# Reciprocals of the attention denominators by way of DRAM instead of spread products, and output stores on another queue

## The chip, the cores and the metric

One core of one Trainium2 chip runs the kernel. The metric is the device time of one execution in microseconds (us). The kernel before took 2346.55 us (median of 3 runs, 2340.79 to 2351.91).

## What is computed

The input is 8 images of 256 channels and 48x48 pixels, in fp32. The first layer is an attention over pixels with 8 heads and a residual (phase L0 of the kernel). The second layer is a linear attention of 64 heads of 8 channels: 32 heads on a 1x1 projection of the image, 32 on that projection after a 5x5 depthwise convolution and a grouped 1x1 product. Cut to what matters here:

```python
qkv = einsum('oc,bchw->bohw', w_qkv, x)
qkv_ms = concatenate([qkv, aggreg(qkv, w_dw, w_pw)], axis=1)     # two sources of 32 heads
q, k, v = relu(...), relu(...), ...                              # per head, 8 channels each
vk  = einsum('bhdn,bhen->bhde', [v, 1], k)
out = einsum('bhde,bhen->bhdn', vk, q)
out = out[:, :, :-1] / (out[:, :, -1:] + 1e-15)                  # one denominator per head and pixel
y = einsum('oc,bchw->bohw', w_proj, out)
result = batch_norm(y) * gamma + beta + x                        # statistics over all 8 images
```

## The kernel before

Three phases follow one another, each a block with one instruction stream per engine: `phase_l0` (the first layer), `phase_l1` (all of the second but its normalisation), `phase_out` (batch norm, residual, store). The change is in the last two.

`phase_l1` takes the images in order, and each image in six units u = 0 to 5, one per part (k, v or q) and half of the heads. On TensorE a unit is: eight groups `convolve(i, u, j)` of 12 matmuls (the convolution with the grouped product folded into its weights `wc`), eight pairs `project(i, u+2)` for the unit two ahead, and after units 1 to 3 of every image but the first `output(i-1, ...)`, the projection of the previous image, 32 matmuls for two chunks of 384 pixels. VectorE makes the weights `wc` of a unit just before that unit (`weights`, in two halves, from `taps`), and in between computes products of k and v (`spin`). ScalarE empties PSUM.

The attended values are never formed: q is divided by its denominator and then multiplied by one matrix `mt1` that holds vk and the projection. Denominators of image i-1 are made during units 0 of image i: `denominators(i-1, d)` for d = 0, 1, 2, each for two chunks of pixels, puts 128 rows of denominators (4 groups of 32) into the PSUM bank `ao`. `reciprocals` on VectorE turns them into `rcp` (two buffers of 384 columns). Every row must then reach the 8 rows of its head in q. In the kernel before TensorE does that: ScalarE rounds `rcp` to `rhi`, GpSimd makes the rest `rlo = rcp - rhi`, and `spread_out` multiplies a 0/1 matrix `spread` with `rhi` and `rlo`, two matmuls of 384 columns for each of 24 tiles (6 chunks x 4 groups of q rows). `normalize` on VectorE multiplies q by each tile in PSUM. The table `SPREADS` says where they stand: 8 of the 24 pairs between the projections c = 5 to 7 of unit 0, and two behind each convolution group of unit 1. `output` waits for all 24.

SyncE (SP) issues all DMAs of this phase in one order written out by hand: per unit the taps, `lay_store` (convolution results to DRAM in two halves), `lay_load` (back to SBUF in head order), `replicate` (projection of the unit two ahead to DRAM, a wait for its landing, and 2.6 MB back as `rep`), and `store_y`. All waits are on semaphores, in the order of the program of each engine.

After the last image, `denominators`, `reciprocals`, `spread_out` and `output` run with nothing beside them but SP's early loads for the last phase (lines 709 to 712). `phase_out` keeps five buffers; SP loads y and x1 of an image, ScalarE scales, VectorE adds, and GpSimd's queue stores (line 1262) as soon as the sum is there.

Of the kernel before, what the change touches and what calls it, by code (L numbers as in the profile page):

```python
# [11 lines left out]
P = 128  # L12
# [13 lines left out]
NU = 6  # L26
# [488 lines left out]
def phase_l1(nc, dram, sem, bnst, q, x1, work, early):  # L515
# [3 lines left out]
    with ExitStack() as ctx:  # L519
# [3 lines left out]
        def ps(name, shape):  # L523
# [9 lines left out]
        spread = sb("spread", [P, 2, 4, P], F32R)  # L533
# [11 lines left out]
        rhi = sb("rhi", [P, 2, CHUNK], F32R)  # L545
        rlo = sb("rlo", [P, 2, CHUNK], F32R)
# [13 lines left out]
         bc_filled, bc_freed, q_copied, rhi_ready, rlo_ready, spread_ready, y_filled, y_freed, bn_done, y_out) = (  # L560
# [4 lines left out]
                "bc_filled bc_freed q_copied rhi_ready rlo_ready spread_ready y_filled y_freed bn_done y_out").split())  # L565
# [3 lines left out]
        NFIRST, NW = 1, 5  # L569
# [5 lines left out]
        SPREADS = {(0, 5): range(0, 2), (0, 6): range(2, 5), (0, 7): range(5, 8),  # L575
                   **{(1, j): range(8 + 2 * j, 10 + 2 * j) for j in range(NG)}}

        spread_raw = stage.rearrange("p h j n -> p (h j n)")[:, 0:8 * P].rearrange("p (c j h) -> p c j h", c=2, j=4)

# [26 lines left out]
        def bc_bank(i, k):  # L606

            return (cv if i is last_image and k % 4 >= 2 else tr)[:, k % 2]
# [17 lines left out]
        def _(sp):  # L626
# [4 lines left out]
            sp.dma_start(spread_raw, dram["spread"]).then_inc(w_in, 16)  # L631
# [17 lines left out]
            def lay_store(i, u):  # L649

                for h in range(2):
# [18 lines left out]

            def image(i, nxt):
# [43 lines left out]
        def _(pe):  # L715
# [105 lines left out]
            def spread_out(i, ks):  # L821

                for k in ks:
                    c, j = k // 4, k % 4
                    d = c // 2
                    if k % 8 == 0:
                        pe.wait_ge(rhi_ready, i * NDEN + d + 1)
                        pe.wait_ge(rlo_ready, i * NDEN + d + 1)
                    if i is last_image:
                        wait_count(pe, bc_freed, 4 * NCH * i + (k - 3 if k >= 4 else 0))  # L830
                    else:
                        if k == 0:
                            pe.wait_ge(tr_freed, (i + 1) * NTR + DG)
                        wait_count(pe, bc_freed, 4 * NCH * i + (k - 1 if k >= 2 else 0))
                    nc.tensor.matmul(bc_bank(i, k)[:, :CHUNK], spread[:, c % 2, j, :], rhi[:, d % 2, :],
                                     start=True, stop=False)
                    nc.tensor.matmul(bc_bank(i, k)[:, :CHUNK], spread[:, c % 2, j, :], rlo[:, d % 2, :],  # L837
                                     start=False, stop=True).then_inc(bc_filled, 1)

            def output(i, chunks, u):  # L840


                pe.wait_ge(bc_freed, 4 * NCH * (i + 1))
# [3 lines left out]
                for c in chunks:  # L847
                    for m in range(CT):
                        k = 2 * c + m
                        if c >= chunks[0] + 2:  # L850
                            pe.wait_ge(y_freed, 2 * NCH * i + k - 3)
                        for j in range(4):
                            mm = nc.tensor.matmul(y_bank(k)[:, :CHUNK], mt[:, j, m * P:(m + 1) * P],  # L853
                                                  q[:, j, c * CHUNK:(c + 1) * CHUNK], start=(j == 0), stop=(j == 3))
                        mm.then_inc(y_filled, 1)

            def image(i, prev, nxt):


                for u in range(NU):  # L860
                    if u == 0 and not prev:
                        product(i, 0, range(DG))
                    for j in range(NG):
# [9 lines left out]
                        if u == 1 and prev:  # L873
                            spread_out(i - 1, SPREADS[u, j])
# [12 lines left out]
                    for c in range(NG):  # L887
                        if u + 2 < NU or nxt:
                            project(*unit_at(i, u + 2), [c])
                        if u == 0 and prev:  # L890
                            if c == 1:
                                denominators(i - 1, 2)
                            spread_out(i - 1, SPREADS.get((u, c), ()))
# [10 lines left out]
            pe.wait_ge(spread_ready, 1)  # L904
# [8 lines left out]
            spread_out(last_image, range(8))  # L913
            denominators(last_image, 2)
            spread_out(last_image, range(8, 4 * NCH))
# [3 lines left out]
        def _(act):  # L919
# [55 lines left out]
            def round_reciprocals(i, d):  # L975

                act.wait_ge(r_ready, i * NDEN + d + 1)

                wait_count(act, bc_filled, 4 * NCH * i + (8 if d == 2 else 0))
                nc.scalar.copy(rhi[:, d % 2, :], rcp[:, (d % 2) * CHUNK:(d % 2 + 1) * CHUNK]).then_inc(rhi_ready, 1)  # L980

# [18 lines left out]
            def image(i, prev, nxt):  # L1000


                for u in range(NU):
                    if u == 0 and not prev:
                        product(i, 0, range(DG))
                    for j in range(NG):
# [7 lines left out]
                        if u == 1 and j == 0 and prev:  # L1014
                            round_reciprocals(i - 1, 2)
# [12 lines left out]
                    for c in range(NG):  # L1028
                        if u + 2 < NU or nxt:
                            project(*unit_at(i, u + 2), [c])  # L1030
                        if u == 0 and prev and c in (0, 3):
                            round_reciprocals(i - 1, c // 3)
# [13 lines left out]
            nc.scalar.copy(spread[:], spread_raw).then_inc(spread_ready, 1)  # L1046
# [6 lines left out]
            for d in range(NDEN):  # L1053
                round_reciprocals(last_image, d)
# [3 lines left out]
        def _(pool):  # L1058
# [24 lines left out]
            def attend(i):  # L1083

                for d in range(NDEN):
                    pool.wait_ge(rhi_ready, i * NDEN + d + 1)

                    wait_count(pool, bc_filled, 4 * NCH * i + (8 if d == 2 else 0))
                    nc.gpsimd.tensor_tensor(rlo[:, d % 2, :], rcp[:, (d % 2) * CHUNK:(d % 2 + 1) * CHUNK],
                                            rhi[:, d % 2, :].bitcast(F32), ALU.subtract).then_inc(rlo_ready, 1)  # L1090

            for i in range(NIMG):
                if i:
                    masked(i - 1, 3)
                    attend(i - 1)
# [3 lines left out]
            attend(last_image)  # L1099

        @block.vector
        def _(dve):
# [48 lines left out]
            def reciprocals(i, d):  # L1151
                dve.wait_ge(den_filled, i * NDEN + d + 1)
                wait_count(dve, rlo_ready, i * NDEN + (1 if d == 2 else 0))
# [5 lines left out]
            def normalize(i, ks):  # L1159
                for k in ks:  # L1160
                    c, j = k // 4, k % 4
                    dve.wait_ge(bc_filled, 4 * NCH * i + k + 1)
                    qc = q[:, j, c * CHUNK:(c + 1) * CHUNK]
                    nc.vector.tensor_tensor(qc, qc, bc_bank(i, k)[:, :CHUNK], ALU.mult).then_inc(bc_freed, 1)  # L1164
# [12 lines left out]
            def image(i, prev):  # L1177
# [33 lines left out]
            reciprocals(last_image, 0)  # L1211
            reciprocals(last_image, 1)
            normalize(last_image, range(8))
            reciprocals(last_image, 2)
            normalize(last_image, range(8, 4 * NCH))
            statistics(last_image, range(NCH))


def phase_out(nc, dram, sem, bnst, q, x1, early):

    with ExitStack() as ctx:
# [36 lines left out]
        @block.gpsimd  # L1258
        def _(pool):
            for k in range(NIMG):  # L1260
                pool.wait_ge(summed, k + 1)
                pool.dma_start(dram["out"][order[k]], buffers[k % NB][0]).then_inc(store[k % NB], 16)
            for r in range(NB):
                pool.wait_ge(store[r], 16 * len(range(r, NIMG, NB)))

        @block.scalar
        def _(act):
            act.wait_ge(stat, CT + 1)
            nc.scalar.activation(rt[:], ve[:], ACT.Sqrt).then_inc(root, 1)
            act.wait_ge(stat, CT + 9)  # L1270
            for k in range(NIMG):
# [5 lines left out]
                last.then_inc(scaled, 1)  # L1277

# [50 lines left out]
def layouts(inputs):  # L1329
# [49 lines left out]
    j = np.arange(4)  # L1379
    row, half = k[:, None, None, None], NB * np.arange(2)[None, :, None, None]  # L1380
    out["spread"] = ((row // 32 == j[None, None, :, None]) & (row % 32 == half + group[j // 2])).astype(np.float32)
# [23 lines left out]
```

## Time and profile before

| what | value |
|---|---|
| profiled execution, its own time | 2353.07 us |
| span of its instructions | 2351.3 us |
| median of three runs | 2346.55 us |
| PE / DVE / ACT / POOL busy | 91% / 65% / 35% / 9% |
| mean granted TensorE clock | 0.955 |
| DMA, hardware queues / GpSimd's queue, share of 16 engines | 51.1% / 1.9% |

Times inside the profile are us from the span's start. In the profile PE is TensorE's matmuls, PEld its weight loads, DVE VectorE, ACT ScalarE, POOL GpSimd, SP SyncE, and L745 is line 745 of the kernel before. The granted clock is a share of 2.4 GHz.

### The profile page before, as it was taken

How to read it: one execution, taken by the hardware profiler on the slowest of the kernel's cores; microseconds unless marked ns; L12 is line 12 of the kernel's file. 1: busy time of each engine (PE TensorE's matmuls, PEld its weight loads, DVE VectorE, ACT ScalarE, POOL GpSimd, SP SyncE). 2: the span in 40 equal slices, each digit the busy share in tenths (PEclk: the TensorE clock that was granted, in tenths of full speed). 3: DMA queues.
4: the chain of work that ended last, by engine and by line, in shares of the span. 5: the costliest groups of instructions: out<-in, count | busy, mean ns of one | idle time of the engine just before them, and what ended most of it. 6: DMA issues, size and time to landing. Idle time of an engine off the chain costs nothing. (4 is left out here: it accounts for less than half of the span.)

```text
span 2351.3 us, 31988 instructions
## 1 busy us (share of the span) xinstructions
PE 2133.4 (91%) x12680; PEld 1513.9 (64%) x12680; DVE 1530.9 (65%) x2330; ACT 833.4 (35%) x1807; POOL 214.3 (9%) x207
## 2 busy tenths in 40 slices
PE   6999999999698799999999999999999999999810
PEld 6888888889566466666666656666666665665500
DVE  4667766767418849667676794975866679491452
ACT  4434434344233333332342332333333233333142
POOL 2233122331100000000000000000000000000000
PEclk9999999999899899999999999999999999999865
DMA  2201222020376864865686486486577658646578
GB/s 105 81 41 41 81 81 81 1 81 41 126 265 214 289 213 159 287 229 209 231 279 213 181 277 224 173 285 226 197 255 254 206 190 270 223 176 222 231 324 358
DMA packets 137411, 448.14 MB, mean 191 GB/s; under 512 B 6960, under 2 KB 105904, under 8 KB 119216
## 3 DMA queue, kind: packets, MB, share of 16 engines
q1 hardware_dynamic: 136112, 427.24, 51.1%
q0 software_dynamic: 1152, 18.87, 1.9%
q8 instruction: 101, 1.65, 0.3%
q14 instruction: 46, 0.38, 0.0%
HBM read 271.30 MB, written 174.78 MB: 190 GB/s over the span
## 5 line engine op out<-in xcount | busy, mean ns | idle before, releaser
L745 PE MATMUL cv<-work,wc 128*64 128x288 f32 x4608 | 620.4, 414 | 22.6 <-issue 18.4
L745 PEld LDWEIGHTS cv<-work,wc 128*64 128x64 f32 x4608 | 307.7, 137 | 267.9 <-issue 53.3
L726 PE MATMUL pj<-x,wqkv 128*128 128x288 f32 x1536 | 389.4, 410 | 20.3 <-DMA x<-scratch_x 20.3
L726 PEld LDWEIGHTS pj<-x,wqkv 128*128 128x128 f32 x1536 | 288.7, 191 | 114.0 <-issue 39.8
L1130 DVE STREAM_SHUFFLE spun<-work 128x1152 f32<-128x1152 f32 x240 | 345.2, 1444 | 0.1
L955 ACT ACTIVATE work<-cv 128x288 f32<-128x288 f32 x384 | 158.0, 411 | 514.6 <-PE cv L745 508.9
L1136 DVE SCALAR_TENSOR_TENSOR spun<-work,spun 128x1152 f32<-128x1152 f32 x240 | 321.2, 1343 | 0.0
L1111 DVE TENSOR_TENSOR wc<-taps 128x512 f32<-128x512 f32 x288 | 180.3, 689 | 194.9 <-PE cv L745 182.4
L936 ACT COPY work<-pj 128x288 f32<-128x288 f32 x384 | 153.6, 400 | 289.5 <-PE pj L726 288.9
L1164 DVE TENSOR_TENSOR q<-q,tr 128x384 f32<-128x384 f32 x180 | 92.2, 550 | 93.8 <-PE tr L837 93.8
L853 PE MATMUL cv<-q,mt 128*128 128x384 f32 x384 | 127.9, 486 | 1.0 <-DVE q L1164 1.0
L853 PE MATMUL tr<-q,mt 128*128 128x384 f32 x384 | 127.8, 486 | 0.0
L199 PE MATMUL qv<-whi,xhi 128*128 128x512 f32 x288 | 117.1, 407 | 0.0
L781 PE MATMUL tr<-ident,work 128*128 128x128 f32 x708 | 115.2, 284 | 1.5 <-ACT spread L1046 1.5
L762 PE MATMUL vk<-kvT 128*128 128x129 f32 x708 | 113.2, 284 | 1.5 <-ACT kvT L967 0.3
L408 POOL TENSOR_TENSOR qs<-qs,qrc 128x512 f32<-128x512 f32 x72 | 75.2, 1049 | 428.4 <-DVE qrc L458 428.4
L201 PE MATMUL qv<-whi,xlo 128*128 128x512 f32 x288 | 113.2, 393 | 0.0
L781 PEld LDWEIGHTS tr<-ident,work 128*128 128x128 f32 x708 | 78.9, 142 | 53.1 <-issue 51.5
L200 PE MATMUL qv<-wlo,xhi 128*128 128x512 f32 x288 | 112.4, 390 | 0.0
L1077 POOL TENSOR_TENSOR vkm<-mask,vkd 128x128 f32<-128x128 f32 x15 | 6.7, 447 | 1141.8 <-DVE vkd L1149 1141.8
L199 PE MATMUL kx<-qnhi,mthi 128*128 128x256 f32 x288 | 91.3, 317 | 16.1 <-DVE mtlo L500 16.0
L853 PEld LDWEIGHTS tr<-q,mt 128*128 128x128 f32 x384 | 73.0, 190 | 50.9
(112 smaller groups left out, 2996.8 us busy)
## 6 DMA issues: line engine op xcount, KB each, us to landing
work<-scratch_padded SPq DMA_DIRECT2D x48, 2599.5 KB, 10.6
scratch_padded<-work SPq DMA_DIRECT2D x48, 1300.0 KB, 6.5
scratch_phases<-work SPq DMA_DIRECT2D x96, 576.0 KB, 5.1
work<-scratch_phases SPq DMA_DIRECT2D x64, 576.0 KB, 5.2
x<-scratch_x SPq DMA_DIRECT2D x9, 2304.0 KB, 10.4
scratch_x<-xs SPq DMA_DIRECT2D x8, 2304.0 KB, 6.9
q<-scratch_phases SPq DMA_DIRECT2D x32, 576.0 KB, 4.6
xs<-in_x SPq DMA_DIRECT2D x7, 2304.0 KB, 9.1
```

Source lines behind the costliest of these rows:

```text
L199: nc.tensor.matmul(out, lhi, rhi, start=start, stop=False, skip_group_check=True)
L201: return nc.tensor.matmul(out, llo, rhi, start=False, stop=stop, skip_group_check=True)
L726: mm = nc.tensor.matmul(pj[:, c % 2, :PLANE], wqkv[:, kc, u, :], x1[:, kc, c * PLANE:(c + 1) * PLANE], start=(kc == 0), stop=(kc == CT - 1))
L745: mm = nc.tensor.matmul(cv[64 * b:64 * b + 64, j % 2, :PLANE], wc[:, 2 * j + b, dy].rearrange("p c o -> p (c o)"), window, start=(dy == 0) ...
L762: mm = nc.tensor.matmul(vk[:, 0:P + 1], kvT[:, g % 2, 0, t, 0:P], kvT[:, g % 2, 1, t, :], start=(g == 0 and t == 0), stop=(g == last and t ...
L781: mm = nc.tensor.transpose(tr[:, g % 2, (2 * kv + t) * P:(2 * kv + t + 1) * P], src, ident[:])
L853: mm = nc.tensor.matmul(y_bank(k)[:, :CHUNK], mt[:, j, m * P:(m + 1) * P], q[:, j, c * CHUNK:(c + 1) * CHUNK], start=(j == 0), stop=(j == 3))
L936: nc.scalar.copy(inner(u % 2, c), pj[:, c % 2, :PLANE].rearrange("p (r c) -> p r c", c=PX)).then_inc(pj_freed, 1)
L955: nc.scalar.activation(stage[:, j // 4, j % 4], cv[:, j % 2, :PLANE], ACT.Copy if PARTS[u] == 2 else ACT.Relu).then_inc(cv_freed, 1)
L1111: op = nc.vector.tensor_tensor(wc[:, blocks, dy], taps[:, u % 2, blocks, 0:DIM].rearrange("p g (c o) -> p g c o", o=1).to_broadcast([P, HB ...
L1130: nc.vector.stream_shuffle(spun[:, t % 2], vc[:, piece], SPINS[t % DIM]).then_inc(spun_ready, 1)
L1136: nc.vector.scalar_tensor_tensor(out=spun[:, t % 2], in0=kc[:, piece], scalar=1.0, in1=spun[:, t % 2], op0=ALU.mult, op1=ALU.mult, accum_o ...
```

## The change

`spread`, `rhi`, `rlo`, the two operations that make them, `spread_out` and `SPREADS` are gone, with the load of the matrix at the start. `normalize` now multiplies q by SBUF tiles of 1536 columns, 6 per image (two groups of q rows by two chunks each) instead of 24 of 384. The tiles come through DRAM: SP stores each `rcp` in two halves into `scratch_recip`, laid out head by head, and loads it with every head's row repeated for its 8 channels. In steady state there are two tiles, `bcb`; for the last image tiles 2 to 5 lie in tensors no longer needed. In `phase_out` the stores are issued by ScalarE, each behind the scaling of the next image; the SBUF that GpSimd's DMAs reserve is cut to 256 bytes.

```diff
+            def store_reciprocals(i, d):
+                sp.wait_ge(r_ready, i * NDEN + d + 1)
+                wait_count(sp, bc_freed, NCH * i)
+                for source in range(2):
+                    sp.dma_start(dram["recip"][d, source].rearrange("h r n -> r h n"),
+                                 rcp[64 * source:64 * source + 64, (d % 2) * CHUNK:(d % 2 + 1) * CHUNK]).then_inc(rc_out[d], 16)
+
+            def load_reciprocals(i, n):
+                d, source = n // 2, n % 2
+                sp.wait_ge(rc_out[d], 32 * (i + 1))
+                if i != last_image:
+                    wait_count(sp, bc_freed, NCH * i + (n - 1 if n >= 2 else 0))
...
+                rows, tile = dram["recip"][d, source], bc_tile(i, n)
+                if source == 0:
+                    sp.dma_start(tile, bass.AP(rows.tensor, rows.offset, [[0, DIM], [4 * CHUNK, NB], [1, 4 * CHUNK]])
+                                 ).then_inc(bc_in[n], 16)
+                else:
+                    for h in range(2):
+                        sp.dma_start(tile[h:P:2], bass.AP(rows.tensor, rows.offset + HB * h * 4 * CHUNK, [
+                            [4 * CHUNK, HB], [0, DIM], [1, 4 * CHUNK]])).then_inc(bc_in[n], 16)
@@ SP, image(i)
-                    lay_store(i, u)
+                    lay_store(i, u, [0])
+                    if u == 1 and i:
+                        load_reciprocals(i - 1, 4)
+                        load_reciprocals(i - 1, 5)
+                    lay_store(i, u, [1])
...
+                    if u == 0 and i:
+                        for d in range(NDEN):
+                            store_reciprocals(i - 1, d)
+                        load_reciprocals(i - 1, 0)
+                        load_reciprocals(i - 1, 1)
...
                     if u + 2 < NU or nxt:
                         replicate(*unit_at(i, u + 2))
+                    if u == 0 and i:
+                        load_reciprocals(i - 1, 2)
+                        load_reciprocals(i - 1, 3)
@@ SP, after the last image, ahead of the early loads
+            for d in range(NDEN):
+                store_reciprocals(last_image, d)
+                load_reciprocals(last_image, 2 * d)
+                load_reciprocals(last_image, 2 * d + 1)
@@ PE, output
-                pe.wait_ge(bc_freed, 4 * NCH * (i + 1))
...
+                    pe.wait_ge(bc_freed, NCH * i + 2 * (c // 2 + 1))
@@ DVE
-            def normalize(i, ks):
...
+            def normalize(i, ns):
+                for n in ns:
+                    d, source = n // 2, n % 2
+                    dve.wait_ge(bc_in[n], (16 + 16 * source) * (i + 1))
+                    qc = q[:, 2 * source:2 * source + 2, d * 2 * CHUNK:(d + 1) * 2 * CHUNK]
+                    nc.vector.tensor_tensor(qc, qc, bc_tile(i, n).rearrange("p (j n) -> p j n", j=2), ALU.mult
+                                            ).then_inc(bc_freed, 1)
@@ DVE, image(i)
-                    normalize(i - 1, range(12))
                 weights(i, 1, [1])
                 if prev:
-                    normalize(i - 1, range(12, 4 * NCH))
+                    normalize(i - 1, range(NCH))
                 weights(i, 2)
@@ phase_out, ACT
+            def store_out(k):
+                act.wait_ge(summed, k + 1)
+                act.dma_start(dram["out"][order[k]], buffers[k % NB][0]).then_inc(store[k % NB], 16)
...
                 last.then_inc(scaled, 1)
+                if k:
+                    store_out(k - 1)
+            store_out(NIMG - 1)
```

## Rows read from the trace of the kernel before

**Rows 1.** The profile's page: busy time by engine; granted clock in 40 slices.
```profile
PE 2133.4 (91%) x12680; PEld 1513.9 (64%) x12680; DVE 1530.9 (65%) x2330; ACT 833.4 (35%) x1807; POOL 214.3 (9%) x207
...
PEclk9999999999899899999999999999999999999865
```

**Rows 2.** Busy time in one image; last three figures: granted clock, DMA share, GB/s.
```profile
858.30:1052.20 193.90, 193.14 (x1143) 122.16 (x1141) 139.97 (x210) 66.10 (x173) 5.66 (x12) 1.00 0.67 230
```

**Rows 3.** Groups by line: shapes, count | busy us, mean ns | idle before, releaser.
```profile
L1164 DVE TENSOR_TENSOR q<-q,tr 128x384 f32<-128x384 f32 x180 | 92.2, 550 | 93.8 <-PE tr L837 93.8
...
L835 PE MATMUL tr<-rhi,spread 128*128 128x384 f32 x180 | 73.7, 410 | 8.1 <-DVE q L1164 6.3 <-issue 1.8
...
L837 PE MATMUL tr<-rlo,spread 128*128 128x384 f32 x180 | 61.4, 341 | 0.0
...
L1307 DVE TENSOR_TENSOR work<-work 128x4608 f32<-128x4608 f32 x4 | 19.7, 4956 | 23.2 <-ACT work L1276 23.2
```

**Rows 4.** Timeline of PE, image 1: start us, us, engine, line, operation, count.
```profile
854.51 4.15 PE L726 MATMUL pj<-x,wqkv 128*128 128x288 f32 x16
858.28 0.55 PE L835 MATMUL tr<-rhi,spread 128*128 128x384 f32 x1
...
864.45 1.68 PE L745 MATMUL cv<-work,wc 128*64 128x288 f32 x12
...
884.35 7.92 PE L726 MATMUL pj<-x,wqkv 128*128 128x288 f32 x32
892.11 5.32 PE L853 MATMUL cv<-q,mt 128*128 128x384 f32 x16
...
902.63 1.68 PE L745 MATMUL cv<-work,wc 128*64 128x288 f32 x12
...
944.65 11.88 PE L745 MATMUL cv<-work,wc 128*64 128x288 f32 x96
```

**Rows 5.** Timeline of DVE in the same stretch.
```profile
855.24 2.55 DVE L1157 RECIPROCAL work<-work 128x384 f32<-128x384 f32 x1
...
885.14 3.70 DVE L1111 TENSOR_TENSOR wc<-taps 128x512 f32<-128x512 f32 x6
891.72 0.01 DVE L1130 LOAD_MASK_SELECT spun<-work  x1 [2.89 <-DMA work<-scratch_phases]
```

**Rows 6.** Timeline of SP's DMA issues in the same stretch.
```profile
848.26 3.31 SPq L668 DMA_DIRECT2D work<-scratch_phases  x2
863.36 0.37 SPq L640 DMA_DIRECT2D scratch_padded<-work  x1
869.42 0.53 SPq L646 DMA_DIRECT2D work<-scratch_padded  x1
```

**Rows 7.** DMA issues of the run: count, KB each, median us to landing.
```profile
work<-scratch_padded SPq DMA_DIRECT2D x48, 2599.5 KB, 10.6
...
scratch_y<-q SPq DMA_DIRECT2D x21, 768.0 KB, 8.2
...
wkqv<-in_wkqv SPq DMA_DIRECT2D x1, 768.0 KB, 4.3
```

**Rows 8.** Busy time by stretch, columns as in Rows 2: one behind an idle TensorE, one of early loads.
```profile
801.20:815.70 14.50, 14.50 (x97) 8.44 (x97) 14.33 (x22) 2.88 (x7) 0.00 (x0) 0.81 0.83 286
...
2190.00:2200.00 10.00, 7.81 (x40) 4.77 (x44) 9.84 (x12) 1.02 (x2) 2.00 (x2) 0.71 1.01 431
```

**Rows 9.** Timeline of PE: idle us before, and its releaser, in brackets.
```profile
654.69 1.06 PE L781 MATMUL tr<-ident,work 128*128 128x128 f32 x8 [1.48 <-ACT spread L1046]
...
801.19 14.51 PE L745 MATMUL cv<-work,wc 128*64 128x288 f32 x96 [12.28 <-issue]
...
1796.04 2.81 PE L745 MATMUL cv<-work,wc 128*64 128x288 f32 x12 [2.68 <-DMA work<-scratch_padded]
...
2211.88 5.43 PE L853 MATMUL cv<-q,mt 128*128 128x384 f32 x16 [1.02 <-DVE q L1164]
```

**Rows 10.** Timeline of the end: SP's first early load, ScalarE's last scaling.
```profile
2187.03 0.34 SPq L710 DMA_DIRECT2D work<-scratch_y  x1
...
2333.06 4.50 ACT L1276 ACTIVATE work<-work,sh,sc 128x2304 f32<-128x2304 f32 x2 [10.89 <-DMA work<-scratch_x]
```

More of the change, by code:

```diff
@@ L544, in phase_l1 @@
         mt = sb("mt1", [P, 4, C])
-        rhi = sb("rhi", [P, 2, CHUNK], F32R)
-        rlo = sb("rlo", [P, 2, CHUNK], F32R)
+        bcb = sb("bcb", [P, 2, 4 * CHUNK])
         spun = sb("spun", [P, 2, SPIN])
@@ L568, in phase_l1 @@
         lay_stored, lay_done = ((lay_stored0, lay_stored1), (lay_stored2, lay_stored3)), ((lay_done0, lay_done1), (lay_done2, lay_done3))
-        NFIRST, NW = 1, 5
+        rc_out = [sem(f"l1_rc_out{d}") for d in range(NCH // 2)]
+        bc_in = [sem(f"l1_bc_in{n}") for n in range(NCH)]
+        NFIRST, NW = 1, 4
         last_image = NIMG - 1
@@ L604, in groups_of, with bc_tile @@
             return DG if PRODUCTS[p][1] == 0 else AG
-        def bc_bank(i, k):
-            return (cv if i is last_image and k % 4 >= 2 else tr)[:, k % 2]
+        def bc_tile(i, n):
+            if i == last_image and n >= 2:
+                spare = (wc.rearrange("p b y c o -> p (b y c o)"), spun.rearrange("p t n -> p (t n)"),
+                         wqkv.rearrange("p k u m -> p (k u m)"))[0 if n < 4 else n - 3]
+                first = (n % 2) * 4 * CHUNK if n < 4 else 0
+                return spare[:, first:first + 4 * CHUNK]
+            return bcb[:, n % 2]
         def y_bank(k):
@@ L647, in replicate, with lay_store @@
                     rows.tensor, rows.offset, [[NB * PADDED, P // 2], [1, 2], [1, NB * PADDED - 1]])).then_inc(rep_in[u % 2], 16)
-            def lay_store(i, u):
-                for h in range(2):
+            def lay_store(i, u, halves=range(2)):
+                for h in halves:
                     sp.wait_ge(cv_freed, i * (NU * NG) + u * NG + 4 * (h + 1))
@@ L819, in denominators @@
                 mm.then_inc(den_filled, 1)
[L821 to L838, printed above, removed]
             def output(i, chunks, u):
-                pe.wait_ge(bc_freed, 4 * NCH * (i + 1))
                 if u is not None:
@@ L1045, in _ @@
             act.wait_ge(w_in, 16 * NW)
-            nc.scalar.copy(spread[:], spread_raw).then_inc(spread_ready, 1)
             image(0, False, True)
@@ L1052, in _ @@
             project_product(last_image, 3)
-            for d in range(NDEN):
-                round_reciprocals(last_image, d)
             output(last_image, range(NCH))
@@ L1210, in _ @@
                 image(i, True)
[L1211 to L1216, printed above, removed]
+            for d in range(NDEN):
+                reciprocals(last_image, d)
+            for d in range(NDEN):
+                normalize(last_image, range(2 * d, 2 * d + 2))
+                if d:
+                    statistics(last_image, range(2 * d - 2, 2 * d))
+            statistics(last_image, range(NCH - 2, NCH))
 def phase_out(nc, dram, sem, bnst, q, x1, early):
@@ L1256, in _ @@
                 sp.dma_start(x, dram["x1"][order[k]]).then_inc(loaded, 16)
[L1258 to L1264, printed above, removed]
         @block.scalar
         def _(act):
+            def store_out(k):
+                act.wait_ge(summed, k + 1)
+                act.dma_start(dram["out"][order[k]], buffers[k % NB][0]).then_inc(store[k % NB], 16)
             act.wait_ge(stat, CT + 1)
@@ L1277, in _ @@
                 last.then_inc(scaled, 1)
+                if k:
+                    store_out(k - 1)
+            store_out(NIMG - 1)
+            for r in range(NB):
+                act.wait_ge(store[r], 16 * len(range(r, NIMG, NB)))
         @block.vector
@@ L1378, in layouts @@
     out["headsel"] = (group.T[:, :, None, None] + NB * np.arange(2)[:, None] == np.arange(32)).astype(np.float32)
-    j = np.arange(4)
-    row, half = k[:, None, None, None], NB * np.arange(2)[None, :, None, None]
-    out["spread"] = ((row // 32 == j[None, None, :, None]) & (row % 32 == half + group[j // 2])).astype(np.float32)
     return {n: np.ascontiguousarray(v) for n, v in out.items()}
@@ L1398 @@
     dram["phases"] = nc.dram_tensor("scratch_phases", (2, NG, P, PLANE), F32).ap()
+    dram["recip"] = nc.dram_tensor("scratch_recip", (NCH // 2, 2, NB, 4, CHUNK), F32).ap()
     dram["out"] = nc.dram_tensor("out_0", (NIMG, P, CT, HW), F32, kind="ExternalOutput").ap()
```

44 lines of the change are left out of this document (8 added, 36 removed).

## The prediction

> **What bounds the kernel now.** I read the page first: TensorE is busy 91% of the span and its granted clock is at the upper level almost throughout, so it sets the time [rows 1]. Then busy time by image: the period is 193.9 us and PE is busy for 193.1 of it, DVE for 140, and the DMA engines are busy 0.67 of it, 230 GB/s [rows 2]. So a microsecond taken from PE in the second phase is worth one, as long as DVE and the transfers still arrive before PE asks. How late they may be is read from the timelines, below. The last 100 us are another thing: PE has ended, and ScalarE's last scaling waits for a DMA [rows 10].
>
> **What the change removes from PE.** 8 spread pairs stand between projections in unit 0, 16 between convolutions in unit 1. Unit 1: the eight groups of convolutions run from 864.45 to 884.35, 19.90 us; the same 96 matmuls with nothing between take 11.8 (944.65, 11.88) [rows 4]: 8.1 us. Unit 0: from 858.28 to 864.45, 6.17 us, only two of the eight projection pairs are left, and eight in a row take 7.92, so 1.97 for two [rows 4]: 4.2. Together 12.3 us per image, seven images, 86 us (the durations of the two lines add to 135, since matmuls overlap [rows 3]). Unhindered, PE would come to unit 2 of image 1 at 902.63 - 12.3 = 890.3.
>
> **What it removes and adds elsewhere.** DVE: 24 products of 0.55 (13.2 us) [rows 3] become 6 of 1536 columns; the sums of 4608 columns take 4.96, so 1.65 each, 9.9 in all, with no wait for PE between. ScalarE and GpSimd lose three short operations per image; neither bounds anything there. SP gains 6 stores (96 KB each) and 9 DMAs that load 6 tiles of 768 KB per image, 4.7 MB, some 13% more bytes than the image's 230 GB/s x 193.9 us = 44.6 MB read and written; engines busy 0.67 have room. It is not the room but the order that costs.
>
> **The cost of one load.** No row shows a load like it: all transfers before have 64 or 128 rows as the outermost count on both sides, the new ones 8 on the DRAM side (and 4 for the stores). Lower bound: `wkqv`, the same 768 KB in the same rows of 6144 bytes, landed in 4.3 us with nothing ahead [rows 7]; at the 431 GB/s of a full queue [rows 8] its bytes are 1.8 of that, the other 2.5 fixed. Upper bound: the y stores, 768 KB amid the image's traffic, 8.2 [rows 7], so 5.7 of transfer. Neither row is plainly nearer: one has the shape of the row, the other the company. I take the middle, 3.7.
>
> A rule of the Trainium skill speaks here: "DMA: Bandwidth & Descriptors", section "Why a DMA increments its semaphore by 16 and not by 1", says that a DMA is spread over the largest number of engines, up to 16, that divides the outermost count of both sides. That is 8 engines for these loads; 8 of 16 at 431 GB/s make 3.65 us of transfer, an estimate by that page that falls on the middle. Were all 16 used it would be 1.8, the first rival. No run here shows it yet.
>
> **The chain of waits in image 1.** Transfers of SP are taken to run one behind the other.
> - Reciprocals 2 are ready at 857.8 [rows 5]. SP, free since 851.6 [rows 6], has waited for them; its two stores (0.37 each) end at 858.5. Transfers start about 1 us later, half a microsecond for the stores (0.2 at full rate to 1.8), so load 0 moves 860.0 to 863.7, load 1 to 867.4, and they are in SBUF 1.5 later. Products 0 and 1 end at 870.5; `output` wants them at 879.9. Covered.
> - `replicate` of unit 2, issued at 863.36 and landed at 869.42 before [rows 6], now stands behind 1.5 MB: landed at 872.2. The load of `rep` (10.6 [rows 7], some 9.3 to its last byte) moves until 881.5.
> - Loads 2 and 3 are issued behind it: last bytes 885.2 and 888.9; products 2 and 3 end at 888.3 and 892.0.
> - SP then waits for these, since tile 4 takes the buffer of tile 2: load 4 is issued at 888.4, stands behind the taps and a `lay_store` (0.8 MB, 2.0 us) and moves 890.9 to 894.6; load 5 to 898.3, landed 899.8, product 5 ends at 901.5.
> - DVE is in order: `weights(i, 2)` stood at 885.14 [rows 5]. Now its first half ends at 901.5 + 1.9 = 903.4. PE, there at 890.3, waits 13.1 us.
> - After an idle of 12.28 us 96 matmuls took 14.51 instead of 11.88, at a granted clock of 0.81, that is, part of it at the lower level, 1.2 GHz [rows 8, 9]; after 2.68 idle, 12 took 2.81 instead of 1.68 [rows 9]. I add 2.7.
>
> So unit 2 starts effectively at 903.4 + 2.7 = 906.1 instead of 902.63 [rows 4]: +3.5 us per image, +24.5 for seven. With 1.8 of transfer the same chain gives 892.9 + 1.1 = 894.0, -8.6 per image; with 5.7, 915.4 + 2.7, +15.5.
>
> Queued behind SP's waits for products 2 and 3: the second half of `lay_store` (unit 1), its `lay_load` and `replicate` of unit 3. The kva data then land at about 905 instead of 891.7 [rows 5], just when DVE is ready for `spin`; `weights(i, 3)` follows 32 us of DVE work later, at 938, while PE asks for it 42 us after unit 2's start (944.65 - 902.63 [rows 4]), at 948. Covered, by 10 us; later units keep their distance, as nothing in them changes.
>
> **Start, end and last phase.** Start: the matrix is not loaded and rounded, for which PE waited 1.48 [rows 9]; -1. After the last image store, load and product are a bare chain instead of rounding and spreading. Output began at 2211.88 [rows 9]; the first two tiles allow it at about 2208, but tiles 2 and 3 come at 2220 and 4 and 5 at 2231, where PE asked for their chunks before at 2222 and 2232: 0. With 1.8 of transfer it is 8 earlier, less 2 of clock. The early loads stood in SP's program at 2187.03 [rows 10] and now stand behind load 5: issued at about 2220, 11.8 MB at 431 GB/s [rows 8], done at 2255, where the last phase starts at 2245 and is bound by DMA: +8 (0 with fast loads). There a store is issued only behind the scaling of the next image, so stores 4 to 6 no longer stand before loads that ScalarE waits for (2333.06 [rows 10]); each is 5.5 us of transfer; some of it comes back at the end, where the last stores queue up: -5 (0 to -8). Sum +2.
>
> Total: +24.5 + 2, about +27. The profiled execution was 2353.07, 6.5 above the median of the runs; from the median, 2346.55 + 27 = 2373.
>
> **Rivals.**
> 1. Loads at full rate (1.8): 7 x -8.6 - 6 - 5 - 1, about -72: 2275. One mechanism: the chain through load 5 ends near 893, so PE waits only 3 us; it decides below about 3.1 us of transfer, where the chain costs what the spreads saved. For it: rows and bytes as in `wkqv`, which is the only row of this row length. Against it: the outermost counts. Chance 0.25.
> 2. The chain and the saving cancel: transfer near 3.1, or part of the queueing overlaps: 2335 to 2358. For it: DMA engines that idle between waits catch up; against: every link is a true dependence. 0.18.
> 3. Loads as slow as the y stores (5.7), since six of them meet `rep` and the taps: +108 and +10: 2465. Against it: those 8.2 us contain waiting of their own. 0.09 for anything over 2410.
>
> The forecast has 0.48, and its own range is 2358 to 2410.
>
> **How the numbers follow.** Half a per cent, 12 us, is about what can be told from no change. Faster: rival 1 and a little of 2, 0.27; same: 0.18; slower: the forecast and rival 3, 0.55. Leaving out the outer half of rival 1 and most of rival 3 gives 2290 to 2410.
>
> **What would show it.** PE: convolutions of unit 1 at 1.475 us each with nothing between, and an idle of 10 to 15 us before unit 2, put down to `wc` (DVE L1111), a granted clock below 1.00 behind it. DMA issues: `bcb<-scratch_recip` at 6 to 8 us from issue to landing. DVE: waits for that DMA before products 2 to 5, of 1.65 each. If the idle before unit 2 is under 5 us, the load was mis-sized and the first rival holds; if PE waits elsewhere, at `output` or unit 3, the chain was drawn wrong; if the last phase starts its loads at 2245 unhindered, the term of +8 falls.

## The result, and the profile after

The changed kernel took 2504.26 us (median of 4 runs, 2500.18 to 2508.97) against 2346.59 for the kernel before (4 runs, 2340.79 to 2351.91): ratio 1.067, 95% interval 1.065 to 1.069. The forecast was 2373, the range ended at 2410. The direction was right, the size far off: +158 us instead of +27.

The page after: busy time by engine, then the granted clock in 40 slices and the DMA packets by size. Rows 1 answer to it.
```profile
span 2507.2 us, 31140 instructions
...
PE 2061.4 (82%) x12296; PEld 1460.1 (58%) x12296; DVE 1515.2 (60%) x2186; ACT 823.9 (33%) x1782; POOL 186.9 (7%) x175
...
PEclk9999999999899979989997997999899799899755
...
DMA packets 147248, 490.04 MB, mean 195 GB/s; under 512 B 7712, under 2 KB 109728, under 8 KB 129056
```
TensorE has 72 us less to do than in [rows 1] and the span is 156 longer. The lines say where it waits: groups of instructions after (count | busy, mean ns | idle before, releaser).
```profile
L787 PE MATMUL cv<-work,wc 128*64 128x288 f32 x4608 | 620.8, 418 | 221.9 <-issue 221.0 <-DMA work<-scratch_padded 0.7
...
L1156 DVE TENSOR_TENSOR q<-q,bcb 128x1536 f32<-128x1536 f32 x44 | 77.4, 1758 | 313.7 <-DMA bcb<-scratch_recip 313.7
```
The convolutions stand idle for 222 us, and VectorE waits 314 us for the new loads: 7.1 us before each of 44 products. The timeline of TensorE, image 1, answers to [rows 4]:
```profile
859.00 11.88 PE L787 MATMUL cv<-work,wc 128*64 128x288 f32 x96
...
888.99 0.27 PE L834 MATMUL ao<-ident,vkm 128*128 128x128 f32 x1
914.52 3.15 PE L787 MATMUL cv<-work,wc 128*64 128x288 f32 x12 [25.26 <-issue]
...
940.93 7.92 PE L768 MATMUL pj<-x,wqkv 128*128 128x288 f32 x32
```
Unit 1 runs its 96 convolution matmuls in 11.88 us with nothing between, TensorE is at unit 2 at 889.3, and there it waits 25 us. The profile names "issue" as the releaser, which here only says that no semaphore event was matched; VectorE's timeline (next) shows what it is: the weights of unit 2 begin at 912.53. Image 1 is the best of the seven:
```profile
1132.92 3.15 PE L787 MATMUL cv<-work,wc 128*64 128x288 f32 x12 [33.45 <-issue]
...
2199.20 3.15 PE L787 MATMUL cv<-work,wc 128*64 128x288 f32 x12 [30.99 <-issue]
```
The seven idles before unit 2 sum to 202.5 us. In the kernel before, unit 2 of the last image starts at 2071.80:
```profile
2071.80 1.68 PE L745 MATMUL cv<-work,wc 128*64 128x288 f32 x12
```
From the starts of unit 2 the 156 us of span add up: 914.52 against 902.63 [rows 4] in image 1 is +11.9; the six periods up to 2199.20 sum to 1284.7 against 1169.2, +115.5; the rest to the end is 308.0 against 279.5, +28.5.

VectorE after, image 1 (start, duration, line, operation, idle before and releaser); [rows 5] answer to it.
```profile
856.03 0.56 DVE L1147 TENSOR_SCALAR work<-ao 128x384 f32<-128x384 f32 x1 [3.33 <-DMA scratch_recip<-work]
856.62 2.55 DVE L1149 RECIPROCAL work<-work 128x384 f32<-128x384 f32 x1
859.09 1.82 DVE L1103 TENSOR_TENSOR wc<-taps 128x512 f32<-128x512 f32 x3
869.49 1.76 DVE L1156 TENSOR_TENSOR q<-q,bcb 128x1536 f32<-128x1536 f32 x1 [8.57 <-DMA bcb<-scratch_recip]
873.23 1.76 DVE L1156 TENSOR_TENSOR q<-q,bcb 128x1536 f32<-128x1536 f32 x1 [1.99 <-DMA bcb<-scratch_recip]
893.57 1.76 DVE L1156 TENSOR_TENSOR q<-q,bcb 128x1536 f32<-128x1536 f32 x1 [18.58 <-DMA bcb<-scratch_recip]
898.05 1.76 DVE L1156 TENSOR_TENSOR q<-q,bcb 128x1536 f32<-128x1536 f32 x1 [2.72 <-DMA bcb<-scratch_recip]
907.39 1.76 DVE L1156 TENSOR_TENSOR q<-q,bcb 128x1536 f32<-128x1536 f32 x1 [7.58 <-DMA bcb<-scratch_recip]
910.86 1.76 DVE L1156 TENSOR_TENSOR q<-q,bcb 128x1536 f32<-128x1536 f32 x1 [1.71 <-DMA bcb<-scratch_recip]
912.53 3.69 DVE L1103 TENSOR_TENSOR wc<-taps 128x512 f32<-128x512 f32 x6
```
And SP's queue in the same stretch; [rows 6] answer to it.
```profile
850.21 10.04 SPq L675 DMA_DIRECT2D scratch_recip<-work  x6
860.29 0.62 SPq L690 DMA_DIRECT2D bcb<-scratch_recip  x1
...
862.27 0.54 SPq L639 DMA_DIRECT2D scratch_padded<-work  x1
877.02 0.56 SPq L645 DMA_DIRECT2D work<-scratch_padded  x1
877.67 0.59 SPq L690 DMA_DIRECT2D bcb<-scratch_recip  x1
...
895.40 0.59 SPq L690 DMA_DIRECT2D bcb<-scratch_recip  x1
899.89 1.22 SPq L694 DMA_DIRECT2D bcb<-scratch_recip  x2
```
DMA issues after (KB each, median us from issue to landing):
```profile
scratch_padded<-work SPq DMA_DIRECT2D x48, 1300.0 KB, 9.6
scratch_phases<-work SPq DMA_DIRECT2D x96, 576.0 KB, 9.7
```
These two are old transfers; in the kernel before they landed in 6.5 and 5.1 us. Not all of that is due to the new loads: in e1 (below), which has none of them, the same transfers land in 8.8 and 6.4 us. The delay by the loads is plainer in the chain: `replicate` of unit 2, issued at 862.27 right behind loads 0 and 1, has landed by 877.02, 14.8 us, where e1 needs 5.9 (860.21 to 866.12).

### The profile page after: what moved, and what is told of

It reads as the page before. It is cut to its first block and busy times, and to the rows that moved or that the text cites. A ratio compares the mean times of both kernels' runs of the same rounds, so it can differ in the third digit from the quotient of the medians.

```text
span 2507.2 us, 31140 instructions
## 1 busy us (share of the span) xinstructions
PE 2061.4 (82%) x12296; PEld 1460.1 (58%) x12296; DVE 1515.2 (60%) x2186; ACT 823.9 (33%) x1782; POOL 186.9 (7%) x175
## 2 busy tenths in 40 slices
DMA packets 147248, 490.04 MB, mean 195 GB/s; under 512 B 7712, under 2 KB 109728, under 8 KB 129056
## 5 line engine op out<-in xcount | busy, mean ns | idle before, releaser
L787 PEld LDWEIGHTS cv<-work,wc 128*64 128x64 f32 x4608 | 316.5, 139 | 471.4 <-issue 257.8
L768 PE MATMUL pj<-x,wqkv 128*128 128x288 f32 x1536 | 387.6, 410 | 19.8 <-DMA x<-scratch_x 19.8
L1156 DVE TENSOR_TENSOR q<-q,bcb 128x1536 f32<-128x1536 f32 x44 | 77.4, 1758 | 313.7 <-DMA bcb<-scratch_recip 313.7
L876 PE MATMUL cv<-q,mt 128*128 128x384 f32 x384 | 133.9, 504 | 34.3 <-DVE q L1156 34.2
L876 PEld LDWEIGHTS cv<-q,mt 128*128 128x128 f32 x384 | 75.4, 198 | 86.2 <-DVE q L1156 36.1
```

What stands on the lines that cost most here:

```text
L768: mm = nc.tensor.matmul(pj[:, c % 2, :PLANE], wqkv[:, kc, u, :], x1[:, kc, c * PLANE:(c + 1) * PLANE], start=(kc == 0), stop=(kc == CT - 1))
L787: mm = nc.tensor.matmul(cv[64 * b:64 * b + 64, j % 2, :PLANE], wc[:, 2 * j + b, dy].rearrange("p c o -> p (c o)"), window, start=(dy == 0) ...
```

## The experiments

Each run stands beside runs of the kernel before on the same chip (2345 to 2349 us). e1 to e4, e8 and e11 are single runs; four runs of the changed kernel spread over 9 us, ten of e10 over 29. e1 to e4 and e11 don't compute the reference.

### e1: the transfers taken out

```diff
-                        for d in range(NDEN):
-                            store_reciprocals(i - 1, d)
-                        load_reciprocals(i - 1, 0)
...
+            nc.gpsimd.memset(bcb[:], 1.0)
```


> Left out: the reciprocals are neither stored nor loaded; q is multiplied by two tiles set to one at the start. My theory (the saving on TensorE is as worked out, all of the loss is the transfers): unit 2 starts 12.3 us earlier per image than before, no idle of TensorE over 3 us ahead of it, 7 x 12.3 = 86 less plus about 8 at the end and 5 in the last phase: about 2250 us. Rival (the larger products on VectorE or the changed order cost time of their own): above 2290.

Measured: 2252.65 us. TensorE goes into unit 2 of image 1 without a stall:
```profile
889.68 0.27 PE L819 MATMUL ao<-ident,vkm 128*128 128x128 f32 x1
889.88 1.68 PE L772 MATMUL cv<-work,wc 128*64 128x288 f32 x12
```
So removing the spread products is worth what the prediction said (86 us, and some 7 at start and end), and all of the loss, 252 us from here to 2504, comes with the stores and loads of the reciprocals and the waits for them.

### e2, e3, e4: the width of the load and the repeated rows, apart

The changed kernel's load has 8 as its outermost count on the DRAM side and reads each row 8 times. Three more source patterns of the same bytes in the same rows of 6144 make a two by two table. For source 0 (source 1 likewise):
```diff
-  bass.AP(rows.tensor, rows.offset, [[0, DIM], [4 * CHUNK, NB], [1, 4 * CHUNK]])        after: 8 outermost, each row 8 times
+  bass.AP(rows.tensor, rows.offset, [[CT * HW, P], [1, 4 * CHUNK]])                     e2: 128 outermost, 128 rows
+  bass.AP(rows.tensor, rows.offset, [[4 * CHUNK, NB], [0, DIM], [1, 4 * CHUNK]])        e3: 16 outermost, each row 8 times
+  bass.AP(rows.tensor, rows.offset, [[17 * CT * HW, DIM], [CT * HW, NB], [1, 4 * CHUNK]])  e4: 8 outermost, 128 rows
```


> Left out: the tiles are loaded from rows of the layer's input instead of the reciprocals; same bytes, same number of DMAs, but 128 (or 64) different DRAM rows as the outermost count. Theory W (8 engines instead of 16 make the load slow): marginal time of a tile falls from 3.8 to about 2.2 us, idle of TensorE ahead of unit 2 from 27 to about 12, total about 2385. Theory R (many reads of the same few DRAM rows are slow, whatever the engines): the same result here, since the rows are different as well. If neither is the cause: 2504.

> Left out: the rows go to the wrong heads. The outermost count of the source is 16, each reciprocal row is still read 8 times. Theory W: as the run with different rows, about 2385, small packets in the page fall by 72 x 8 less than before the change by 16 per DMA instead of 8. Theory R: stays near 2504, a tile at 3.8 us or more.

> Left out: the tiles are loaded from rows of the layer's input. 128 different DRAM rows with 8 as the outermost count. Theory W: near 2504, DMA share about 0.5 while only such a load runs, a tile at 3.8 us. Theory R: about 2385, as with 16 engines.

| us | 128 different rows | each row 8 times |
|---|---|---|
| outermost 16 or more | 2348.80 (e2) | 2387.28 (e3) |
| outermost 8 | 2492.92 (e4) | 2504.26 (after) |

Width is worth 144 us with different rows and 117 with repeated ones; repetition 38 us and 11 us. The 11 us are hardly more than the spread of the runs. And e2 and e4 read rows of the layer's input, while e3 and the changed kernel read rows stored just before, so "each row 8 times" carries this difference with it. Of the numbers expected, e3 and e4 met theory W; e2 came out 36 us under its 2385. The idle before unit 2 of image 1, in e2, e3 and e4:
```profile
902.14 3.15 PE L786 MATMUL cv<-work,wc 128*64 128x288 f32 x12 [10.54 <-issue]
```
```profile
903.17 3.15 PE L786 MATMUL cv<-work,wc 128*64 128x288 f32 x12 [11.60 <-issue]
```
```profile
912.41 3.15 PE L786 MATMUL cv<-work,wc 128*64 128x288 f32 x12 [25.30 <-issue]
```
After the last image the new loads run with little beside them, and the traces show their rate there (tile: 768 KB at this rate, an estimate):

| run, stretch in us | GB/s | DMA share | us for a tile |
|---|---|---|---|
| e2, 2197 to 2200 | 369 | 0.95 | 2.1 |
| e3, 2231 to 2236 | 251 | 1.03 | 3.1 |
| e4, 2318 to 2328 | 157 | 0.50 | 5.0 |
| after, 2328 to 2342 | 118 | 0.47 | 6.7 |

The stretches are short, that of e2 above all (its 5 us from 2196 give 305 at 0.85). The narrow loads keep half of the engines busy. Repeated rows are slower at either width, with the engines no less busy or hardly so. A tile's load on 16 engines that starts there lands in 4.3 us with different rows (e2), like `wkqv`, and in 5.8 with repeated ones (e3). Amid the traffic of the images the load of a whole tile lands 5.7 us after its issue in e2 and 7.3 in e3 (medians of 22); for e4 and after the profile has no landing.

The page's count of small packets shows the width too; e3:
```profile
DMA packets 147824, 490.04 MB, mean 205 GB/s; under 512 B 8288, under 2 KB 110304, under 8 KB 129632
```
After has 7712 packets under 512 B, the kernel before 6960, 752 fewer. If a DMA ends with one small packet on each engine it uses, 48 stores on 4 engines and 72 loads on 8 make 192 + 576 = 768, less 16 for the matrix that is no longer loaded: 752. In e3 the same bytes have 8288, that is 576 = 72 x 8 more: 16 engines. The Trainium skill, "DMA: Bandwidth & Descriptors", section "Why a DMA increments its semaphore by 16 and not by 1", states the rule that the forecast named: the engines of a DMA are the largest number up to 16 that divides both outermost counts, and the last thing on each is the increment of the semaphore. The traces agree: 752 and 576 packets, and shares of 0.47 and 0.50 against 0.95 and more.

### e6: the output stores on ScalarE's queue, alone

```diff
-        @block.gpsimd
...
-                pool.dma_start(dram["out"][order[k]], buffers[k % NB][0]).then_inc(store[k % NB], 16)
...
+                if k:
+                    store_out(k - 1)          # ScalarE, behind the scaling of image k
```


> The kernel before with the output stores on ScalarE's queue alone. Theory: the last load lands some 5 us earlier since stores 4 to 6 start later, -3 to -5 us: 2342. Rival (ScalarE is held up by its waits for sums): +3 or more. No effect: within 2 us.

Measured: 2343.98 against 2346.52, ratio 0.9994 (0.9981 to 1.0006). No effect that can be measured.

### e8: four tiles instead of two

```diff
-        bcb = sb("bcb", [P, 2, 4 * CHUNK])
+        bcb = sb("bcb", [P, 4, 4 * CHUNK])
...
+            return bcb[:, n % 4]
```


> The changed kernel with four tiles for the reciprocals instead of two, so that SP waits for no product. Theory (order and slow loads): products 4 and 5 come some 3 us earlier per image, about 2480. Rival (the wait for a free tile is the cause): idle ahead of unit 2 under 15 us, total below 2430.

Measured: 2507.98 against the 2480 of the theory; the rival is out too. SP no longer waits for products 2 and 3 before it issues loads 4 and 5. SP and VectorE of e8:
```profile
881.98 3.77 SPq L691 DMA_DIRECT2D bcb<-scratch_recip  x1
```
```profile
910.07 1.76 DVE L1157 TENSOR_TENSOR q<-q,bcb 128x1536 f32<-128x1536 f32 x1 [7.98 <-DMA bcb<-scratch_recip]
```
Load 4 is issued 13.4 us earlier than in the changed kernel (895.40), and its product comes 2.7 us later (907.39 there). So nothing is gained by the free tile: the load waits for the transfers ahead of it either way.

### e5: the same transfers, but the weights no longer behind them

```diff
@@ DVE, image(i)
-                    normalize(i - 1, range(NCH))
-                weights(i, 2)
+                    normalize(i - 1, range(0, 2))
+                weights(i, 2)
...
+                    normalize(i - 1, range(2, 4))       # after the first six rotations of spin
...
+                    normalize(i - 1, range(4, 6))       # after weights(i, 3)
@@ SP: loads 4 and 5 in unit 2
```


> Complete and exact; narrow loads kept. VectorE makes the weights of unit 2 right after the first two products, products 2 and 3 come after six rotations of unit 2, products 4 and 5 after the weights of unit 3; loads 4 and 5 are issued in unit 2. My theory (the loads cost only because VectorE's order puts them ahead of the weights of unit 2): TensorE's idle ahead of unit 2 goes from 27 us to under 2, period 182 us, total 2252.7 (the run without transfers) plus the end with its loads, about 35 more: 2288. Rival (the narrow loads take so much of the DMA engines that other transfers come late): an idle of 5 us or more shows up elsewhere in each image, total above 2325.

Measured: 2462.45, ratio 1.050 (1.048 to 1.052): 42 us less than after, 174 more than I expected. The rival was right. Unit 2 now starts at once, and stops some 5 us later. TensorE, ScalarE and VectorE of e5:
```profile
887.88 1.68 PE L787 MATMUL cv<-work,wc 128*64 128x288 f32 x12
...
901.33 1.23 PE L804 MATMUL vk<-kvT 128*128 128x129 f32 x4 [8.98 <-ACT kvT L984]
...
1005.77 6.58 PE L787 MATMUL cv<-work,wc 128*64 128x288 f32 x30 [8.93 <-issue]
```
```profile
900.32 0.41 ACT L972 ACTIVATE work<-cv 128x288 f32<-128x288 f32 x1 [11.41 <-DMA scratch_phases<-work]
```
```profile
873.79 3.70 DVE L1103 TENSOR_TENSOR wc<-taps 128x512 f32<-128x512 f32 x6
908.35 0.01 DVE L1122 LOAD_MASK_SELECT spun<-work  x1 [30.87 <-DMA work<-scratch_phases]
```
ScalarE can't reuse the buffer whose store to DRAM still stands in the queue, and VectorE waits 31 us for data that the queue brings late. These are transfers of the kernel before. In SP's program loads 2 and 3 are issued just ahead of that store (876.53 to 878.5, the store at 879.11); that they hold it up is read from this order.

### e7: e5 with the spread products kept for the last image

```diff
+            spread_out(range(8))             # last image only
...
-                normalize(last_image, range(2 * d, 2 * d + 2))
+            normalize_last(range(8))
```


> Complete and exact. As the reordered kernel, but the last image keeps the spread products with rhi and rlo. Theory (the end costs 35 us because store, load and product are a bare chain there and the early loads stand behind it): about 30 us less than the reordered kernel, about 2256. Rival (the end is bound by the bytes of the last phase anyway): within 8 us of the reordered kernel.

Measured: 2432.96, ratio 1.037 (1.035 to 1.038), 29.5 less than e5, as expected. At the end nothing covers the transfer, which is plain in the changed kernel (VectorE's products 0 and 1 stand at 2335.82 and 2341.71 behind an issue at 2326.11), and while they are awaited the loads move with little beside them. One stretch of after (us, busy time of PE, PEld, DVE, ACT, POOL, then granted clock, DMA share, GB/s):
```profile
2328.00:2342.00 14.00, 0.00 (x0) 0.00 (x0) 3.38 (x3) 0.00 (x0) 0.00 (x0) 0.50 0.47 118
```
118 GB/s with half of the DMA engines busy: at this rate a tile of 768 KB takes 6.7 us (estimate; the two products stand 5.9 apart). TensorE stands still for it (the first and the last of three):
```profile
2343.52 7.01 PE L876 MATMUL cv<-q,mt 128*128 128x384 f32 x16 [19.59 <-DVE q L1156]
...
2382.49 8.00 PE L876 MATMUL cv<-q,mt 128*128 128x384 f32 x16 [9.79 <-DVE q L1156]
```

### e11: e5 with the wide source of e3

```diff
-  [[0, DIM], [4 * CHUNK, NB], [1, 4 * CHUNK]]
+  [[4 * CHUNK, NB], [0, DIM], [1, 4 * CHUNK]]
```


> Left out: the rows go to the wrong heads. The reordered kernel, loads still on SP's queue, with 16 as the outermost count of the source. Theory (narrow loads hold up what stands behind them on SP's queue): the loss against the reordered kernel shrinks by more than half, about 2330. Rival (the order on SP's queue matters, not the width): above 2400.

Measured: 2374.51, 88 less than e5. Neither number was met: of the 210 us that e5 stands over e1, 88 go with the width and 122 stay. Its idles that are left stand ahead of units 3 and 4 (3.8 and 7 to 9 us per image).

### e9, e10: a queue of their own

```diff
-                sp.dma_start(tile, ...)
+                pool.dma_start(tile, ...)            # GpSimd issues stores and loads
...
+                    pool.wait_ge(cv_filled, i * (NU * NG) + 2 * NG + 1)     # unit 2 has begun
+                    load_reciprocals(i - 1, 2)
```


> Complete and exact. The reordered kernel with all stores and loads of reciprocals issued by GpSimd on its own queue, tiles 2 and 3 when unit 2 has begun, tiles 4 and 5 when its convolutions are done. Theory Q (in the reordered kernel the loads stood on SP's queue ahead of the stores of the convolution results, ScalarE then waited 11.4 us for the staging buffer, and VectorE 31 us for k and v): the waits of ScalarE and VectorE for these go back to those of before, period 182 to 186 us, total about 2300, end included. Rival (bytes on the engines, whichever queue): as the reordered kernel, 2440 or more.

> Complete and exact. The same with the spread products kept for the last image. Theory Q: another 15 to 30 us less, about 2270, clearly faster than the kernel before. Rival: 2410 or more.

Measured: e9 2372.05, ratio 1.010 (1.007 to 1.014); e10 2341.01 (10 runs, 2325.22 to 2353.82), ratio 0.997 (0.995 to 0.999). e9 is 90 us under e5 with loads of the same shape: the queue was changed, the loads come later, and the SBUF that GpSimd's DMAs reserve is 4096 bytes instead of 256; these were not told apart. Both fall short of what the theory wanted by 70 us. The groups of e10 say what is left:
```profile
L750 PE MATMUL cv<-work,wc 128*64 128x288 f32 x4608 | 622.5, 420 | 74.5 <-issue 71.9 <-DMA work<-scratch_padded 2.2 <-ACT work L952 0.4
```
75 us of idle before convolutions instead of 222. The `bcb` loads land after 14.2 us in e10; the old transfers are slow too (`scratch_padded<-work` 10.7, `scratch_phases<-work` 11.9; in e5 10.5 and 11.5). So the old transfers land no sooner than in e5, and still TensorE's idle before the products of k and v (`vk<-kvT`), 66 us in e5, is 1.5 us in e9 and e10: a second queue takes the loads out of SP's order, but does not make the transfers beside them faster.

### e12: the wide load made exact

```diff
-                for source in range(2):
+                for source, copy in ((0, 0), (0, 1), (1, 0), (1, 1)):      # each reciprocal stored twice
...
+                    for part in range(4):
+                        pool.dma_start(tile[32 * part:32 * part + 32],
+                                       bass.AP(rows.tensor, rows.offset, [[4 * CHUNK, 2 * NB], [1, 4 * CHUNK]]))
```


> The kernel of e10 (reordered, the reciprocals' DMAs issued by GpSimd, spread products kept for the last image), with loads whose outermost count is 32 or 16 instead of 8. Each reciprocal is stored twice over, so that the load of source 0 can be four DMAs of 32 different rows each and that of source 1 two DMAs with an outermost count of 16; the result is the reference's. Four stores instead of two per pair of chunks. Theory (the width of a load costs wherever it is issued, because the rows behind it on the same engines wait): in e11 the wide loads took 88 us off e5; in e10 part of that queueing is already gone, so I expect 30 to 45 us less than e10's 2341: about 2300, with the landing of the bcb loads under 10 us instead of 14.2 and the idles ahead of unit 4 (6 to 9 us) halved. Rival (what holds the loads up on this queue is not their width but the queue's own issue and the traffic beside it): within 10 us of 2341, landings of bcb still over 12 us; with the six issues more per image it may also be slower.

Measured: 2331.61 (2327.71 to 2335.28), ratio 0.993 (0.991 to 0.995), the fastest version that computes the reference: 17 us under the kernel before, beside which it ran (2348.82). Groups and DMA issues of e12:
```profile
L750 PE MATMUL cv<-work,wc 128*64 128x288 f32 x4608 | 613.2, 415 | 36.3 <-issue 36.3
...
L853 PE MATMUL cv<-q,mt 128*128 128x384 f32 x384 | 137.1, 513 | 34.9 <-DVE q L1196 33.6 <-DVE q L1251 1.2
```
```profile
bcb<-scratch_recip POOLq DMA_DIRECT2D x84, 192.0 KB, 7.6
bcb<-scratch_recip POOLq DMA_DIRECT2D x42, 384.0 KB, 10.9
```
The idle before convolutions is half as long (75 to 36 us), but `output` now waits for its products, 35 us against 15 in e10. The profile of e10 is of its slowest run (2353.8), that of e12 of a usual one, so the groups show more than the 9 us between the medians. That gain, not 30 to 45, is small: the ratios' intervals (0.995 to 0.999 and 0.991 to 0.995) just touch. Besides the width, the number of stores and loads and the count of times that a row is read changed too, so the run does not show what the width alone is worth on this queue. In image 1 the first load is issued 4.3 us later than in e10, behind twelve stores (866.89 against 862.57), and product 1 stands 11.5 us later (889.06 against 877.51): the longer row of issues explains less than half of that.

## Why the prediction was wrong

**"What the change removes from PE" held.** Unit 1 in 11.88 us, unit 2 reached at 889.3 (forecast 890.3), e1 at 2253.

**"The chain of waits in image 1" ended where it was drawn to end, and was priced wrong.** Its links and the wait at the end of it are found in the trace:

| link | forecast | measured |
|---|---|---|
| stores issued | 858.5 | 860.25 |
| products 0 and 1 done | 870.5 | 875.0 |
| `replicate` landed (`rep` issued) | 872.2 | 877.0 |
| products 2 and 3 done | 888.3, 892.0 | 895.3, 899.8 |
| load 4 issued | 888.4 | 895.4 |
| product 5 done | 901.5 | 912.6 |
| idle before unit 2 | 13.1 | 25.3 |

One link was none: SP's wait for product 2 before load 4. Without it (e8) the load is issued 13.4 us earlier and its product comes no sooner.

**The step that failed is "The cost of one load": the term of 3.7 us.** Where the loads run with little beside them they take 6.7 us each (118 GB/s); in the chain product 0 stands 9.2 us behind its load's issue where the forecast had 6.7, product 4 12.0 instead of 7.7. I had halved the engines of `wkqv` and kept all the rest. The experiments say what the term is made of: with 16 engines and different rows it is 2.1, with repeated rows 3.1, with 8 engines 5.0 and 6.7. The upper bound of 5.7, given 0.09, was still too low, and by the forecast's own sum it gives 2465.

**That the right price would have met the result is luck.** The forecast's sum gives 2275, 2373 and 2465 for a term of 1.8, 3.7 and 5.7. Read between and beyond these, 6.7 gives about 2511, and 2504 was measured. But 2.1 (e2) gives 2290 for a measured 2349, 3.1 (e3) 2342 for 2387, 5.0 (e4) 2433 for 2493: 45 to 60 us too low. In image 1, with 6.7, the chain would end some 6 us later than it does.

**What no term held.** (1) The third reciprocal overwrites the buffer of the first and waits until that has been stored: 3.33 us in image 1 (VectorE's first line above), 6.24 in image 2; the forecast took it at its old time. (2) Old transfers beside the new ones: in e2, whose loads are wide and plain, `replicate` of unit 2 still takes 11.0 us to land (864.06 to 875.05) where e1 needs 5.9. (3) Image 1 was taken for all; in the six others the idle is 27.4 to 33.4 us. The clock, taken at 2.7, costs 2.6: unit 2 from 914.52 to 940.93 is 26.4 us at a granted clock of 0.90, in e1 from 889.88 to 913.73 23.85 us at 1.00. A mean idle of 29.5 over the six, less the 12.3 saved, with the 2.6, gives 19.8 per image, and the periods show 19.3.

**"Covered, by 10 us" for `spin` and unit 3 held only by accident.** After the change no unit but the second waits for long. e5 took the wait before it away, and others appeared (8.98, 2.77 and 8.93 us in image 1): the 25 us that TensorE loses at unit 2 had hidden them.

**The end.** 0 for the bare chain and +8 for the early loads became +28.5 altogether; e5 and e7 price it at 29.5. Counted from unit 2 of the last image, `output` begins at 144.3 us against 140.1 before, so the first two tiles come nearly as forecast. The others don't: products 0, 2 and 4 stand at 2335.82, 2352.57 and 2371.92, 17 to 19 us apart, where the forecast had 11 to 12, and the last chunks of `output` begin at 183.3 (2382.49) against 160.8 before. The early loads begin at 163.3 (2362.47) against 115.2 [rows 10], 48 us later where the forecast had 33. The stores on ScalarE, -5 (0 to -8), are -2.5 by e6, which can't be told from nothing.

Two slips of its arithmetic change nothing: loads and stores of the reciprocals are 12% of 44.6 MB, not 13, and two stores of 96 KB take 0.46 us at 431 GB/s, not 0.2.

**The rivals.** Rival 1 (full rate) is refuted for the change as it stands by the packet count and by the rate of its loads. Its condition was tried: e2 and e3, loads on 16 engines, still wait 7.6 to 16.5 us before unit 2 and take 2349 and 2387, not 2275. So even with the width right the sum was too kind, and e2 still stands 96 us above e1 with plain, wide transfers; that this is their queueing is argued from the idles, not shown by a run. Rival 3 had the direction of the error, for another reason: it put the slowness down to the traffic, and the loads are slow without it.

**Open.** Why a repeated row is slower to read, and whether it is the repetition or the fresh store; why the sum is 45 to 60 us too low for e2, e3 and e4 but not for the change; how much of e9's gain is the queue and how much the later loads; what the width is worth on GpSimd's queue; and what of the 79 us between e12 and e1 an order of issues could still take, for e1 also lacks the transfers of the end.

## What to carry to other kernels

Before work goes from the bound engine to a DMA, look at the outermost count of both sides: 8 instead of 16 cost this kernel 117 to 144 us. Then write the chain as issue, landing, next issue through the queue it shares, and give every old transfer behind it the new delay too, not only the new ones. Where no row shows such a transfer, a single run of it would have priced the term before the sum was made. When one stall hides others, take it away in an experiment before believing that the others are covered.

## What the runs showed of the hardware

- Loads of 768 KB tiles in rows of 6144 bytes with little beside them: outermost count 8 and each row read 8 times 118 GB/s at an engine share of 0.47; with different rows 157 at 0.50 (e4); outermost 16 or more and repeated rows 251 at 1.03 (e3), with different rows 369 at 0.95 (e2). So engines that are busy all the time moved a third less when the rows repeated.
- Two products in a row tell little of that: at the end they stand 2.7 us apart in e2 and 2.8 in e3, 3.7 in e4 and 5.9 in after.
- The product of 1536 columns took 1.76 us, the forecast from 4608 columns was 1.65.
- "issue" as a releaser covered a plain wait for VectorE's weights: 202.5 of its 221 us, the seven idles before unit 2.
